# Six shared expert blocks ahead of the routed ones, 32 weight pieces split in the attention stage, and an earlier bias load

## The reference, cut to what matters

```python
x = x + xattn(layernorm(x), ctx)
x = x + attn(layernorm(x), Wqkv, bqkv, Wo, bo)     # ... vals @ Wo.T + bo
xf = layernorm(x)
logits = xf @ router_w + router_b                  # top 2 of 8, softmax -> gates
expert(xf, w1, w3, w2) = silu(xf @ w1) * (xf @ w3) @ w2
x = x + sum_e gates[e] * routed_e(xf) + shared_0(xf) + shared_1(xf)
```

## Time and profile before

| | |
|---|---|
| median of 3 runs | 899.88 us (896.88 to 900.57) |
| the profiled execution's own time | 903.94 us |
| its span, first to last instruction | 902.2 us, mean granted TensorE clock 0.929 |
| busy in the span | PE 762.0 (84%), PEld 637.8, DVE 588.6 (65%), ACT 365.7, POOL 167.7 |
| head attention / experts | about 693 to 772 / 772 to 902 us of the span |

### The profile page before, as it was taken

How to read it: one execution, slowest core, us unless ns; L and a number is a source line. 1 busy time by engine, 2 the same in 40 slices (tenths; PEclk the granted TensorE clock), 3 DMA queues, 4 the chain that set the end, 5 groups by cost and what they waited for, 6 DMA issues and landing times. The chain is left out here.

```text
span 902.2 us, 38766 instructions
## 1 busy us (share of the span) xinstructions
PE 762.0 (84%) x17710; PEld 637.8 (71%) x17710; DVE 588.6 (65%) x1131; ACT 365.7 (41%) x736; POOL 167.7 (19%) x441
## 2 busy tenths in 40 slices
PE   5697879998989998988998889798887697659994
PEld 2545879998989987988997889697664564324442
DVE  3987456876785875785876785646476576773234
ACT  3875515334434333434334431102177564252230
POOL 3020211311312211311211311102002024140003
PEclk9899889999999999999999999989979568969997
DMA  9989960364390572491563480701366900644515
GB/s 337 379 170 179 250 102 4 67 89 164 64 224 34 80 136 104 49 220 51 79 117 124 68 177 4 143 4 49 114 219 181 303 7 1 210 141 99 136 59 152
DMA packets 177951, 114.77 MB, mean 127 GB/s; under 512 B 146364, under 2 KB 156660, under 8 KB 174588
## 3 DMA queue, kind: packets, MB, share of 16 engines
q1 hardware_dynamic: 167148, 99.94, 46.0%
q10 hardware_dynamic: 8640, 6.56, 2.5%
q0 software_dynamic: 2000, 5.80, 2.1%
HBM read 61.94 MB, written 12.85 MB: 83 GB/s over the span
## 5 line engine op out<-in xcount | busy, mean ns | idle before, releaser
L1062 PE MATMUL banks<-qa,ctxT 128*128 128x64 f16 x3744 | 119.3, 195 | 22.8 <-issue 11.2
L1062 PEld LDWEIGHTS banks<-qa,ctxT 128*128 128x128 f16 x3744 | 115.8, 99 | 25.1 <-issue 11.9
L1013 PEld LDWEIGHTS banks<-wall,whhT 128*128 128x128 f16 x3456 | 107.4, 98 | 11.3 <-issue 5.5
L1013 PE MATMUL banks<-wall,whhT 128*128 128x64 f16 x3456 | 109.9, 193 | 4.8 <-issue 4.8
L1013 PE MATMUL banks<-qa,wall 128*128 128x64 f16 x3456 | 106.8, 194 | 4.6 <-issue 4.4
L1013 PEld LDWEIGHTS banks<-qa,wall 128*128 128x128 f16 x3456 | 104.2, 99 | 5.4 <-issue 4.7
L1081 PEld LDWEIGHTS banks<-qa,wall 128*128 128x128 f16 (+1 forms) x1872 | 89.2, 100 | 10.4 <-issue 10.3
L1081 PE MATMUL banks<-wall 128*128 128x64 f16 (+1 forms) x936 | 89.0, 196 | 5.4 <-issue 5.4
L1081 PE MATMUL banks<-qa,wall 128*128 128x64 f16 (+1 forms) x1872 | 90.1, 196 | 4.1 <-DVE wall L787 2.3
L1081 PEld LDWEIGHTS banks<-wall 128*128 128x128 f16 (+1 forms) x936 | 85.2, 100 | 0.0
L568 ACT ACTIVATE wall<-wall 128x832 f32<-128x832 f32 x24 | 21.5, 897 | 123.2 <-DVE wall L766 123.2
(11 more groups left out here) (289 smaller groups left out, 1487.1 us busy)
## 6 DMA issues: line engine op xcount, KB each, us to landing
wall<-in_ctx_dram SPq DMA_DIRECT2D x17, 1024.0 KB, 10.3
wall<-in_L_ffn_routed_w_dram SPq DMA_DIRECT2D x23, 512.0 KB, 7.8
unit<-in_ctx_dram SPq DMA_DIRECT2D x6, 1024.0 KB, 7.9
xg_scratch<-room SPq DMA_DIRECT2D x1, 3840.0 KB, 18.2
y_scratch<-room ACTq DMA_DIRECT2D x15, 256.0 KB, 2.1
ctxT<-in_L_xattn_gru_wih_dram SPq DMA_DIRECT2D x3, 1024.0 KB, 17.3
ctxT<-in_L_xattn_gru_whh_dram SPq DMA_DIRECT2D x1, 3072.0 KB, 26.0
ctxT<-in_L_attn_Wqkv_dram SPq DMA_DIRECT2D x12, 256.0 KB, 8.3
```

The costliest lines, as they stand in the source:

```text
L1013: mm = pe.matmul(dst[o], a, b, start=start, stop=True, skip_group_check=True)
L1062: mm = pe.matmul(score[n][:, t * K:(t + 1) * K], a, q, start=(k == 0), stop=(k == 3 * DC - 1), skip_group_check=True)
```

## The change

- `LATE` goes from 4 to 2: six shared blocks stand ahead of the routed ones, two behind them. With `FIRST` = 6, `drained` has six entries instead of eight.
- `IN_HEADS` goes from 28 to 32 and `TWICE` = 2 is new: in the head loop two pieces are split where one was, ten in all instead of five; behind the loop two and eight instead of two and nine. The experts have 16 pieces left, spread over six blocks.
- Experts 5 and 6 are loaded by SyncE within `head_attention`, once q, v and the last scores have been read; `experts` loads expert 7 alone.
- The bias row's load moves from the head of `head_attention`'s SyncE list into that of `project_qkv`, behind the load of `Wo` and ahead of the fold copies. Its place in memory is the same.

```diff
-IN_HEADS = 28
+IN_HEADS = 32
+TWICE = 2
...
             sp.dma_start(wo_raw, dram.Wo.rearrange("(c p) d -> p c d", p=P)).then_inc(wo_in, 16)
+            sp.dma_start(h.bo_row, dram.bo.partition_broadcast(P)).then_inc(h.bo_in, 16)
             for j in range(NJ):
...
-        bo_row = late[:, 2 * GB * HD:2 * GB * HD + D]
...
         @block.sync
         def _(sp):
-            sp.dma_start(bo_row, dram.bo.partition_broadcast(P)).then_inc(bo_in, 16)
             load_expert(sp, dram.routed, 0, raw_of(e_all.wall, 0), e_all.wall_in[0])
...
             sp.dma_start(e_all.rb_row[:], dram.router_b.partition_broadcast(P)).then_inc(e_all.r_in, 16)
+            sp.wait_ge(h.q_ready, B)
+            sp.wait_ge(v_ready, B)
+            sp.wait_ge(scored, B)
+            for n in range(EARLY, NE - 1):
+                load_expert(sp, dram.routed, n, raw_of(e_all.wall, n), e_all.wall_in[n])
...
                 if 2 <= k < B - 1:
-                    wall_high(act, e_all, IN_PROJECT + k - 2, IN_PROJECT + k - 1)
+                    wall_high(act, e_all, IN_PROJECT + TWICE * (k - 2), IN_PROJECT + TWICE * (k - 1))
             vals_high(B - 1)
-            wall_high(act, e_all, IN_PROJECT + B - 3, IN_PROJECT + B - 1)
+            wall_high(act, e_all, IN_PROJECT + TWICE * (B - 3), IN_PROJECT + TWICE * (B - 3) + 2)
             for t in range(2):
                 tile_high(act, e_all, turn_bank(t), t)
-            wall_high(act, e_all, IN_PROJECT + B - 1, IN_HEADS)
+            wall_high(act, e_all, IN_PROJECT + TWICE * (B - 3) + 2, IN_HEADS)
...
-                dve.wait_ge(bo_in, 16)
+                dve.wait_ge(h.bo_in, 16)
                 for t in range(RT):
-                    dve.tensor_tensor(rows[:, t], rows[:, t], bo_row, ALU.add).then_inc(bo_added, 1)
+                    dve.tensor_tensor(rows[:, t], rows[:, t], h.bo_row, ALU.add).then_inc(bo_added, 1)
...
                 if k >= 3:
-                    wall_low(dve, e_all, IN_PROJECT + k - 3, IN_PROJECT + k - 2)
+                    wall_low(dve, e_all, IN_PROJECT + TWICE * (k - 3), IN_PROJECT + TWICE * (k - 2))
...
-        LATE = 4
+        LATE = 2
...
-            for n in range(EARLY, NE):
-                load_expert(sp, dram.routed, n, raw_of(wall, n), wall_in[n])
+            load_expert(sp, dram.routed, NE - 1, raw_of(wall, NE - 1), wall_in[NE - 1])
             sp.wait_ge(scattered, 2 * RT * 16)
...
+        h.bo_row = heads[:, HC * ROWS + 2 * GB * HD:HC * ROWS + 2 * GB * HD + D]
+        h.bo_in = sem("t_bo_in")
```

More of the change, by code:

```diff
@@ L1532, in head_attention @@
         pT_chunks = pT.rearrange("p s g (h c ii r) -> p s g ii h c r", h=2, ii=4, r=4)
-        bo_in, zeroed, v_ready, v_turned, v_out, expd, prob_out, prob_turned, pT_out, valued, \
+        zeroed, v_ready, v_turned, v_out, expd, prob_out, prob_turned, pT_out, valued, \
             vals_hi, vals_lo, y_done, y_out, bo_added, dve_done = (sem(n) for n in (
-                "bo_in", "zeroed", "v_ready", "v_turned", "v_out", "expd", "prob_out", "prob_turned",
+                "zeroed", "v_ready", "v_turned", "v_out", "expd", "prob_out", "prob_turned",
                 "pT_out", "valued", "vals_hi", "vals_lo", "y_done",
@@ L1687, in _ @@
                 if k >= 3:
-                    wall_low(dve, e_all, IN_PROJECT + k - 3, IN_PROJECT + k - 2)
+                    wall_low(dve, e_all, IN_PROJECT + TWICE * (k - 3), IN_PROJECT + TWICE * (k - 2))
             vals_low(B - 1)
             add_y(RT - 2)
-            wall_low(dve, e_all, IN_PROJECT + B - 3, IN_PROJECT + B - 1)
+            wall_low(dve, e_all, IN_PROJECT + TWICE * (B - 3), IN_PROJECT + TWICE * (B - 3) + 2)
             for t in range(2):
                 tile_low(dve, e_all, turn_bank(t), t)
-            wall_low(dve, e_all, IN_PROJECT + B - 1, IN_HEADS)
+            wall_low(dve, e_all, IN_PROJECT + TWICE * (B - 3) + 2, IN_HEADS)
             add_y(RT - 1)
```

## The result

| | before | changed kernel |
|---|---|---|
| median of 9 runs each | 900.53 us (896.88 to 904.16) | 893.63 us (890.59 to 897.04) |
| ratio with its 95% interval | | 0.9919 [0.9894, 0.9943] |
| the profiled execution's own time, span | 903.94, 902.2 us | 890.59, 888.8 us |

The change makes the kernel 6.9 us faster (5.1 to 9.5 by the interval), beyond the half per cent that a measurement tells apart. 895.3 was forecast, 890 to 899 as the range. The two profiled executions lie 13.4 us apart, but 3.75 us of that is not the change: the first exponential of the heads, at 693.65 before, comes at 689.90, and the load of `Wo`, which both kernels issue ahead of anything that was edited, was already 3.7 us sooner (654.63 and 650.95). The other 9.65 us are cut into stages in the table of the experiments.

What follows compares the result with a forecast made beforehand. It took VectorE's 7.35 us wait for the bias row as the longest single wait in the heads' chain. Terms -7.35 + 1.0 - 0.75 + 2.5 = -4.6 us took 899.88 to 895.3 us, range 890 to 899.

Steps and rivals of the forecast that it cites:

- the bias row: Heads: VectorE's wait for the bias row's load disappears, -7.35 us; its issue in the projection costs 0 (0 to 0.5).
- The router's bias: Heads: its load, 0.8 us sooner, becomes the next wait and delays the chain, +1.0 us (ends 0 and 2.0).
- Expert 0: Heads: ScalarE waits 0.2 us for this expert's third load, at most 1.0.
- the twice as many pieces: Head loop: five more split pieces on ScalarE and VectorE cost 0, at most 0.8 us.
- one piece fewer behind the loop: Behind the head loop: eight instead of nine pieces between the two stretches of turned rows, -0.75 us.
- The start of the experts: TensorE's 4.10 us period sets the pace; routed blocks start at 809.8 instead of 807.26, +2.5 us (ends -0.2 and +4).
- The first routed product: Start of routed blocks: after a 2.8 us gap it stays slow at the lower clock, 0 (other end -1.7 us).
- rival 1: Clock helps: held over the 2.8 us gap (893.6 us) or regained in the heads (892.7); chance 0.27 (0.20 and 0.07).
- The end: After the routed blocks: two shared blocks fewer free 8.2 us of TensorE while the gather is awaited anyway, 0.
- Rival 2: Loads replace the bias row's wait: router bias +2.0, expert 0 +0.5, experts' start +3.5, giving 897.8 us; chance 0.17.
- Rival 3: Start of experts: the six shared blocks run at half clock, +11.7 us on top, 907 us; chance 0.06.

Runs made afterwards that it cites:

- run 1: Kernel before with only the bias row's load moved into the projection stage, behind `Wo`'s: median 895.02 us, ratio 0.9919.
- run 5: The changed kernel, unaltered, measured again on another chip: median 892.06 us, ratio 0.9892 to the kernel before.
- run 3: Changed kernel with `LATE` = 4 instead of 2, so four shared blocks ahead of the routed ones: median 892.91 us, ratio 0.9902 to the kernel before.
- run 7: Changed kernel with `LATE` = 4 and 65 waits on TensorE instead of one ahead of the routed blocks: median 891.87 us, ratio 0.989 to before.
- run 4: Changed kernel with `LATE` = 3, so five shared blocks ahead: median 891.84 us, ratio 0.9889 to the kernel before.
- run 8: Changed kernel with five blocks ahead, pieces spread 3, 4, 4, 4, 1, router's weights and bias loaded in the projection: median 888.42 us, ratio 0.9875 to before.
- run 2: Kernel before with only `LATE` = 2, so six shared blocks ahead and 20 pieces in the experts: median 902.19 us, ratio 1.0017.
- run 6: Changed kernel with `LATE` = 4 and the bias row's load back in the heads: median 901.2 us, ratio 0.999 to the kernel before.

## Why the prediction was right, and where it failed

The direction and the size came from the step on **the bias row**: -7.35 forecast, 7.45 us measured at the next normalisation, and run 1 gives with this step alone the ratio of the change's first measurement (0.9919; run 5 gave 0.9892, whose interval takes that in). Its issue in the projection costs nothing, as forecast.

**The router's bias** was forecast at +1.0 and cost 0.2 at block 5's normalisation (7.25 to 7.04). It did become the next wait (0.87 us, 0.98 to 2.04 in runs 1, 3, 5 and 7; run 4 had none), but the load came 1.3 us sooner than before and not 0.8. The step reckoned with the bytes alone; the queue also gave back some of the time of the bias row's issue. In run 3, with the longest wait (2.04 us), block 5's normalisation came 1.2 us later than in the changed kernel and the heads took 0.9 us more (71.80 instead of 70.86): there the term is about what was forecast. In run 1 (1.80 us), where the loop has one piece a block, that normalisation came only 0.1 later; its heads are as long because of the ninth piece behind the loop. In run 8, without the wait, it came 0.4 sooner. The Trainium skill, "DMA: Bandwidth & Descriptors", section "Queues, rings and completion order", has descriptors consumed in ring order on each DMA engine. The traces agree: 7.5 us from issue to landing behind three experts' loads, and in run 8, which puts the load ahead of them, the wait is gone.

**Expert 0**, **the twice as many pieces** and **one piece fewer behind the loop** went as forecast: 0.57 us of wait (0.2 forecast, 1.0 as the end) and 0.2 of it in the chain; no wait of VectorE behind the further pieces; -0.8 for -0.75.

**The start of the experts** was forecast at +2.5 and took +1.0 behind placing (+1.6 for the whole stretch) in the first trace, +2.5 behind placing in run 5. TensorE's period of 4.10 and the 4.4 us from the end of `up(5)` to the routed blocks (4.6 measured, 792.55 to 797.16) held. What scatters is the point from which TensorE sets the pace: `up(3)` ended 6.6 us behind placing and not 8.2, because TensorE idled only 0.81 us ahead of the turn (5.69 before) and then did the turn, block 0's `down` and `up(3)` at the full clock, in 4.13 us instead of 5.86. That the gap was so short is luck: `up(2)` ahead of it had run at the lower clock and ended late. In run 5 it did not, and there the step took what was forecast.

**The first routed product** is where a value was chosen wrongly. The gap was forecast at 2.8 us and is 2.94; the text took the end where the clock falls, 0, and both traces of the changed kernel show the other, -1.7: 2.76 us for 4.46. This is the first half of rival 1. Its second half fell: the heads' projections took 18.1 us before and 17.9 after. By the Trainium skill, "TensorE: Matmul & The Clock Gate", section "What's actually happening", activity releases the throttle. The trace agrees inside the first projection, where the granted clock goes from 0.50 to 1.00 in both kernels; it does not for the work ahead, since from 706 us on TensorE of the changed kernel was busy without a break and stayed at 0.50 until 717. The rival's price was read too low as well: it took 1.3 us for each of the next two projections, which before ran 5.30 and 4.44 us, 2.55 and 1.69 above the 2.75 of the full clock.

**The end** is the step that failed: "Two shared blocks fewer behind them take 8.2 us of TensorE out of a stretch that waits for the gather anyway: 0." It brought -1.6. The late blocks were no bound, as the step said. But their products are a part of TensorE's instruction list, and taking them from behind the last store moved the instruction load that had fallen beside it. This step looked at engines and not at the transfers beside the chain.

Together: -7.9 in the heads, +1.6 at the start, -1.7 and -1.6 make -9.65 for the profiled pair, -6.9 by medians (-10.1 in run 5), -4.6 forecast. So the time lies in the range, but the sum was too small. The two terms that failed are 3.3 us; the clock's had its end in the range, the store's had none. The other 1.8 us, in the heads and at the start, are steps that came out better than forecast, the second by luck. Rival 2 did not come: the router's bias landed sooner than forecast, and expert 0's longer wait left 0.2 us in the chain, not 0.5. Rival 3 did not come: only `up(2)` ran at the lower clock (5.18 us), and `up(3)` to `up(5)` took 2.75.

What the forecast did not see is that six blocks ahead were not needed for its own sum: without them (run 3) the start falls from +1.6 to -1.7, and what the change wins with them, the clock and the store, is not their doing by design.

## What to carry to other kernels

Look for the one wait at which an in-order engine stands with everything behind it, and ask which queue its load stands in: moving one broadcast of a bias row ahead of a 3.84 MB transfer gave 7.0 of the 9.0 to 9.7 us that the two traces of the changed kernel show in the four stages, and by medians nothing beyond it can be told for certain. Before work is put ahead of a stage as a filler, find what that stage waits for when the filler is gone (here the turned rows, 16.7 us behind placing); filler beyond that floor only pushes the start back. And where a step at the very end grows or shrinks by a microsecond for no reason in the code, look at the transfer queues for an instruction load beside it.

## What the runs showed of the hardware

**An instruction load delays the completion of a store beside it.** The same 256 KB store landed in 2.0 us in six traces with no instruction packet beside it, and in 3.3 to 3.8 us in the four traces in which a packet of some 16 KB (140 packets are 2.29 MB) ran beside it; there nine of the store's 144 packets came when the others were done. Nine is as many as one of the 16 engines gets if all get the same, which is an estimate; that this one was the engine that carried the instructions is likely, but not shown. The Trainium skill has two passages that bear on it: "Runtime: NRT & Kernel Launch", section "Instruction fetch mechanics", has instructions fetched in 16 KiB blocks by a DMA queue of the sequencer's own, at a cost that is mostly hidden; "DMA: Bandwidth & Descriptors", section "Queues, rings and completion order", has a transfer's semaphore written only after every earlier write of that DMA engine, across its queues. The packet's size agrees. That the cost is hidden did not hold here: 1.5 us on the chain that ended last. Data itself came late, so whether the order of semaphores adds to it is not shown.

**The clock over a short gap.** Before the first routed product TensorE idled 2.51 us (run 8) and the product then took 4.45; 2.94 us (the changed kernel, twice) and it took 2.76; 3.54 to 4.76 us (runs 2, 3, 4) and it took 5.30; 5.83 to 7.38 us (before, runs 1, 6 and 7) and it took 4.25 to 4.71. In run 8 the granted clock was still 1.00 in the half microsecond ahead of the product and 0.50 a microsecond into it. So the length of the gap alone does not decide whether the clock is held, and what does is open. A kernel's start can win or lose 1.7 to 2.5 us by it.

**A broadcast's issue depends on what is queued.** The bias row's took 1.9 to 2.6 us of SyncE in the projection and 4.6 to 5.5 us at the head of the heads, behind the 3.84 MB; without it there, two loads of an expert took 6.5 to 9.2 us (seven traces), where the bias row and those two had taken 9.4 before. Moving an issue out of such a place frees less of the queue than its own duration: counted from the first exponential, the router's bias was issued 1.5 to 2.6 us sooner for 5.29.
